# Expert layers that return half of the experts' rows by an accumulating indirect DMA into HBM instead of by one-hot products

## What is computed

```python
scores = jnp.einsum('ntd,ed->nte', x, gate_w)
probs = jax.nn.softmax(scores, axis=-1)
g, m = jax.lax.top_k(probs.transpose(0, 2, 1), k)        # each expert picks its own 128 tokens
xin = x[batch_idx, m]                                    # gather: rows of the normed x
h = jnp.einsum('nekd,edf->nekf', xin, w1)
h = jax.nn.gelu(h, approximate=False)
h = jnp.einsum('nekf,efd->nekd', h, w2)
out_tok = g[..., None] * h
out = jnp.zeros((n, t, d), dtype=x.dtype).at[batch_idx, m].add(out_tok)   # scatter: give the rows back
...
x = x + 0.5 * _L1_ffn_ref(_layernorm(x, axis=-1), ...)
```

## Time and profile before

| | us |
|---|---|
| median of 3 runs | 1667.79 (1666.23 to 1670.37) |
| the profiled execution: its own time | 1667.2 |
| its span, first to last instruction | 1665.5 |

### The profile page before, as it was taken

The page is one execution under the profiler, slowest core; times in us unless marked ns, Lnnn a source line. Parts: engine busy times, 40 slices in busy tenths (PEclk is TensorE's granted clock), DMA queues, the critical chain, the costliest instruction groups (busy, mean ns, idle before and its releaser), DMA issues. The chain is left out here.

```text
span 1665.5 us, 40705 instructions
## 1 busy us (share of the span) xinstructions
PE 1446.4 (87%) x12722; PEld 1003.0 (60%) x12722; DVE 1267.3 (76%) x3158; ACT 1160.5 (70%) x2439; POOL 778.2 (47%) x1204
## 2 busy tenths in 40 slices
PE   5999679999999999989970999999878609999998
PEld 2554334445454544435550899999745408999997
DVE  6777478888888888657848677877778586778776
ACT  5888337777777787758842778787566407887785
POOL 4687724545454444434415666554022106665540
PEclk9999759999999999989975899999989658999999
DMA  5022201111111111001012111110001101111110
GB/s 156 29 83 85 86 13 46 41 42 44 42 43 41 45 40 45 5 1 38 26 48 94 40 38 38 32 30 24 1 26 39 38 3 40 51 50 50 49 36 25
DMA packets 84640, 70.92 MB, mean 43 GB/s; under 512 B 16752, under 2 KB 78000, under 8 KB 84528
## 3 DMA queue, kind: packets, MB, share of 16 engines
q1 hardware_dynamic: 76336, 52.62, 11.3%
q0 software_dynamic: 8192, 16.79, 3.8%
HBM read 46.81 MB, written 22.54 MB: 42 GB/s over the span
## 5 line engine op out<-in xcount | busy, mean ns | idle before, releaser
L1111 DVE TENSOR_REDUCE at_negmax<-at_s_ps 128x2 f32<-128x1024 f32 (+3 forms) x384 | 389.4, 1044 | 64.7 <-PE at_s_ps L888 57.4
L1017 ACT ACTIVATE at_p<-at_x_ps 128x512 f32<-128x512 f32 x640 | 355.3, 596 | 98.9 <-PE at_x_ps L900 92.4
L1335 POOL DMA_INDIRECT e_x_in<-xn,e_row_c x256 | 259.2, 1012 | 146.0 <-issue 75.7
L1072 POOL TENSOR_SCALAR_AFFINE_SELECT at_p<-at_p 128x256 f32<-128x256 f32 (+1 forms) x448 | 191.3, 441 | 243.8 <-ACT at_p L1017 243.7
L900 PE MATMUL at_x_ps<-qr,kr 50*128 50x512 bf16 (+3 forms) x1024 | 227.4, 305 | 18.6 <-ACT at_p L1017 10.9
L1458 DVE TENSOR_TENSOR e_hid_lo<-e_hid,e_hid_hi 128x512 fp32r<-128x512 f32 x256 | 177.3, 693 | 86.8 <-ACT e_hid_hi L1422 77.2
L883 PE MATMUL at_s_ps<-kr,qr 48*128 48x512 bf16 (+3 forms) x1024 | 188.3, 312 | 18.3 <-PEq L1679 11.9
L1421 ACT ACTIVATE e_hid<-e_h_ps 128x512 f32<-128x512 f32 x256 | 154.9, 605 | 43.0 <-PE e_h_ps L1363 37.8
L916 PE MATMUL at_o_ps<-at_p,at_va 128*32 128x512 f32 (+3 forms) x2048 | 179.8, 447 | 0.0
L900 PEld LDWEIGHTS at_x_ps<-qr,kr 50*128 50x128 bf16 x1024 | 66.6, 94 | 153.6 <-ACT at_p L1017 136.8
L1363 PE MATMUL e_h_ps<-e_x_hi,w_hi 128*128 128x256 f32 x512 | 156.5, 306 | 0.0
(11 more groups left out here) (210 smaller groups left out, 3392.5 us busy)
## 6 DMA issues: line engine op xcount, KB each, us to landing
qr<-q_parts SPq DMA_DIRECT2D x128, 48.0 KB
kr<-k_parts SPq DMA_DIRECT2D x128, 48.0 KB
xres<-in_x_dram SPq DMA_DIRECT2D x8, 512.0 KB, 8.2
qr<-q_parts SPq DMA_DIRECT2D x128, 32.0 KB
xn<-m_n_xhat SPq DMA_DIRECT2D x16, 256.0 KB
e_x_in<-xn,e_row_c POOLq DMA_INDIRECT x256
xn<-sc_n_xhat SPq DMA_DIRECT2D x16, 256.0 KB
out_dram<-xres SPq DMA_DIRECT2D x16, 256.0 KB
```

Of the source, the lines that this page charges most:

```text
L1017: a.activation(p_sb[g % 2][:, i, :], x_ps[i % 2][:], ACT.Exp, scale=SCALE).then_inc(x_read, 1)
L1072: sel = gp.affine_select(out=part, in_=part, compare_op=ALU.is_ge, fill=0.0, base=0, pattern=[[0, n] for n in part.shape[1:-1]] + [[1, P]] ...
L1111: v.tensor_reduce(out, scored, AX.X, ALU.max, negate=True).then_inc(s_read, 1)
L1335: nc.gpsimd.indirect_dma_start(out=x_in[k][u][:], out_offset=None, in_=xn_dram, in_offset=bass.IndirectOffsetOnAxis(ap=row_c[k][:, u:u + 1 ...
```

## The change

In each turn the experts `k` = 0, 2, 4, 6 (`BY_DMA`) return their rows by DMA, and the experts 1, 3, 5, 7 (`BY_PE`) by one-hot products as before.

- While the tokens are chosen, SyncE writes all of `xres` to two tables in HBM, `sum_dram[0]` for the even and `sum_dram[1]` for the odd sequences (`keep_rows`: 16 DMAs of 256 KB in each expert layer).
- For an item of `BY_DMA` there is no `one_hot`, no `y_hi`, no `y_lo` and no `give_back`. VectorE writes the weighted rows as float32 to `y_row` straight from `y_ps`, and GpSimd issues two indirect DMAs with `compute_op=ALU.add` (`scatter`) that add the 128 rows of each sequence to its table. Each waits for the scatter of the same table that went before it in the turn.
- GpSimd's code is written out in full instead of looped, its gathers take the row numbers straight from `rows` (no `row_c`), and `scatter` of item q-4 stands behind the gather of item q+8 (`LAG`).
- When a turn's last scatter (`k` = 6) has landed, SyncE loads the sequence from the table back into `xres` (`reloaded`: 16 DMAs of 256 KB in each layer), and only then may VectorE add the sum of the other four experts to it. In `e2` the output's stores stand in the same queue behind it.

The core of the diff:

```diff
+BY_DMA = (0, 2, 4, 6)
+BY_PE = tuple(k for k in range(E) if k not in BY_DMA)
...
+        def keep_rows(sp):
+            for n in range(NB):
+                sp.dma_start(of_batch(n), in_chunks(n)).then_inc(sums_set, 16)
...
+                def gather(i, k):
+                    after(pool, t_full, (i - 1) * S + k + 1)
+                    for u in range(U):
+                        at = (i * U + u) * E + k
+                        nc.gpsimd.indirect_dma_start(
+                            out=x_in[k][u][:], out_offset=None, in_=xn_dram,
+                            in_offset=bass.IndirectOffsetOnAxis(ap=rows[:, at:at + 1], axis=0)).then_inc(gathered[k][u], 16)
+
+                def scatter(i, k):
+                    pool.wait_ge(yl_done, i * S + k + 1)
+                    if (i, k) == (0, BY_DMA[0]):
+                        pool.wait_ge(sums_set, NB * 16)
+                    for u in range(U):
+                        if k != BY_DMA[0]:
+
+                            pool.wait_ge(scattered[BY_DMA[BY_DMA.index(k) - 1]][u], i * 16 + 16)
+                        at = (i * U + u) * E + k
+                        nc.gpsimd.indirect_dma_start(
+                            out=sum_dram[u], out_offset=bass.IndirectOffsetOnAxis(ap=rows[:, at:at + 1], axis=0),
+                            in_=y_row[k][:, u, :], in_offset=None, compute_op=ALU.add).then_inc(scattered[k][u], 16)
+
+                LAG = 4
+                for k in range(S):
+                    gather(0, k)
+                for q in range(TU * S + LAG):
+                    if q + S < TU * S:
+                        gather(q // S + 1, q % S)
+                    if q >= LAG and (q - LAG) % S in BY_DMA:
+                        scatter((q - LAG) // S, (q - LAG) % S)
...
                 def give_back(i, k, q):
+                    if k in BY_DMA:
+                        return
                     pe.wait_ge(yl_done, q + 1)
-                    pe.wait_ge(hot_done, q + 1)
-                    if k == 0:
+                    pe.wait_ge(hot_done, i * len(BY_PE) + BY_PE.index(k) + 1)
+                    if k == BY_PE[0]:
...
                 def weigh(i, k, q):
-                    dve.wait_ge(yh_done, q + 1)
+                    if k in BY_DMA:
+                        dve.wait_ge(y_full, q + 1)
+                        dve.wait_ge(cols_done, q * 2 + 2)
+                        for u in range(U):
+
+                            after(dve, scattered[k][u], i * 16)
+                            y = v.tensor_scalar(y_row[k][:, u, :], y_ps[:, u, :], wgt_c[k % 2][:, u:u + 1], None, ALU.mult)
+                        y.then_inc(yl_done, 1)
+                        return
+                    dve.wait_ge(yh_done, i * len(BY_PE) + BY_PE.index(k) + 1)
...
                             dve.wait_ge(o_full, turn * U + u + 1)
+                            dve.wait_ge(reloaded[u], turn * 16 + 16)
                             x = xres[:, turn * U + u, :]
                             v.tensor_tensor(x, o_ps[:], x, ALU.add).then_inc(x_added, 1)
...
+                for n in range(NB):
+                    sp.wait_ge(scattered[BY_DMA[-1]][n % U], n // U * 16 + 16)
+                    sp.dma_start(in_chunks(n), of_batch(n)).then_inc(reloaded[n % U], 16)
```

More of the change, by code:

```diff
@@ L1242, in choose_tokens, with experts_layer @@
     return local, rows, weight
-def experts_layer(nc, sem, h, xres, xn_dram, probs, name, out, weights=None, next_norm=None):
+def experts_layer(nc, sem, h, xres, xn_dram, sum_dram, probs, name, out, weights=None, next_norm=None):
     U = 2
@@ L1259, in experts_layer @@
         two = lambda n, sh, d=F32R: [t(f"{n}{j}", sh, d) for j in range(2)]
-        local, rows, weight = choose_tokens(nc, lambda n, sh, d: tmp.enter_context(nc.sbuf_tensor(n, sh, d)), sem, h, probs, name, weights)
-        row_c = [t(f"row_c{k}", [K, U], U32) for k in range(S)]
+        sums_set = s("sums_set")
+        of_batch = lambda n: sum_dram[n % U][n * T:(n + 1) * T, :].rearrange("(c p) d -> p c d", p=P)
+        in_chunks = lambda n: xres[:, n, :].rearrange("p (c d) -> p c d", c=C)
+        def keep_rows(sp):
+            for n in range(NB):
+                sp.dma_start(of_batch(n), in_chunks(n)).then_inc(sums_set, 16)
+        local, rows, weight = choose_tokens(nc, lambda n, sh, d: tmp.enter_context(nc.sbuf_tensor(n, sh, d)), sem, h, probs, name,
+                                            keep_rows, weights)
         loc_c, wgt_c = two("loc_c", [K, U], F32), two("wgt_c", [K, U], F32)
@@ L1268, in experts_layer @@
         y_hi, y_lo = two("y_hi", [K, U, D]), two("y_lo", [K, U, D])
+        y_row = {k: t(f"y_row{k}", [K, U, D], F32) for k in BY_DMA}
         hot = two("hot", [K, U, T])
@@ L1324, in _ @@
             def _(pool):
[L1325 to L1337, removed]
@@ L1498, in _ @@
             def _(sp):
+                for n in range(NB):
+                    sp.wait_ge(scattered[BY_DMA[-1]][n % U], n // U * 16 + 16)
+                    sp.dma_start(in_chunks(n), of_batch(n)).then_inc(reloaded[n % U], 16)
+                    if out is not None and n % U == U - 1:
+                        for m in range(n - U + 1, n + 1):
+                            sp.wait_ge(x_added, m + 1)
+                            sp.dma_start(out[m].rearrange("(c p) d -> p c d", p=P), in_chunks(m)).then_inc(stored, 16)
                 if out is not None:
-                    with sp.Fori(0, NB) as n:
-                        sp.wait_ge(x_added, n + 1)
-                        sp.dma_start(out[n].rearrange("(c p) d -> p c d", p=P), xres[:, n, :].rearrange("p (c d) -> p c d", c=C)).then_inc(stored, 16)
                     sp.wait_ge(stored, 16 * NB)
@@ L1661, in program @@
         xn_dram = dram("xn", [NB * T, D], F32)
+        sum_dram = [dram(f"sums{u}", [NB * T, D], F32) for u in range(2)]
         xres = sb("xres", [P, NB, T], F32)
```

35 lines of the change are left out of this document (21 added, 14 removed).

## The result

| | before | after |
|---|---|---|
| median of the runs | 1667.07 us | 1706.91 us |
| lowest to highest | 1666.23 to 1670.37 | 1703.19 to 1712.06 |
| ratio, 95% interval | | 1.0239 [1.0221, 1.0257] |

The changed kernel is slower by 40 us. The forecast was 1634 us, with a range up to 1690: the time lies outside it, on the side that had 0.27.

The account below looks back on a forecast made before the run. TensorE, busy 87% of the span, was taken as the bound. Terms: -28.8 - 1.7 + 6.3 + 7.8 = -16.4 us a layer, -32.8 for both, against 1667.2: 1634 us; 8-in-10 range 1606 to 1690.

Parts of the forecast that it names:

- the scatter's issue time: GpSimd's queue: one scatter taken as 1.10 us, range 0.95 to 1.465, with 0.30 us more beside it.
- the scatter's issue is dear: Rival, GpSimd's queue at `scatter`: each 0.1 us more costs 11 us in all; gain eaten at 1.40 us; chance 0.33.
- TensorE's turn without four give-backs: TensorE's slots: 31 give-backs at 0.93 us go, 28.8 us less a layer; a turn falls from 34.6 to 30.9 us.
- The copies: Start of each expert layer: without copies of row numbers the fourth gather starts earlier, 1.7 us less a layer.
- The turn of the queue: GpSimd's queue: 16 x 1.31 + 8 x 1.40 = 32.2 us a turn, 1.3 behind TensorE; 7.8 us over turns 1 to 6.
- The first turn: VectorE's first addition waits for the reload, so TensorE's slot 15 starts late: 6.3 us, once a layer.
- Landing and reload: Behind a turn's last scatter: 3.1 us from its start to landing, then 3.0 us for SyncE's reload of 256 KB.
- SyncE's stores: Stores of `xres` into tables: about 10 us, hidden inside choosing; rival not hidden, up to 5 us a layer, chance 0.05.
- TensorE stays the bound: Rival: GpSimd's queue under 30.9 us a turn and reload in time, so both stalls go, 1606 us; chance 0.15.
- the scatter lands late: Rival, scatters waiting for the preceding expert's: waits begin over 8 us to landing; at 10 us, over 1700; chance 0.07.
- The rule weighed: GpSimd's gathers: had `e_hot` lengthened them, 3 us a layer would come back, 1628 us; the mean was kept.

Follow-up runs that it names:

- group 2: Runs side by side: changed kernel again 1711.12 us; before with loop written out 1667.9; without copies, gathers five ahead 1663.01; two experts, five ahead 1635.43.
- group 1: Runs side by side: changed kernel without reload 1710.6 us, with plain scatters 1727.21, with two experts 1680.1; kernel before without copies, loop written out 1699.6.
- group 3: Changed kernel with gathers five ahead: three experts 1695.43 us, four 1708.55, four with plain scatters 1712.67, four with 64-row adding scatters 1711.87.
- group 5: Four experts, gathers five ahead, plain 32-row scatters: 1625.91 us; kernel before without copies, 32-row gathers eight ahead: 1670.6 us.

## Why the prediction was wrong

**The step that failed is the scatter's issue time.** It was taken as 1.10 us "nearer to the mean" of a gather, with 1.465 as its upper end. It is 1.702. The prediction's own rule for it, 11 us for each 0.1 us, gives 6.0 x 11 = 66 us: 1634 + 66 = 1700, against 1706.9 measured. With the measured turn and first wait in its sum, -28.8 - 1.7 + 12.3 + 6 x (37.4 - 30.9) = 20.8 us a layer, it is 1709. And where a scatter does cost what was forecast (plain, 32 rows, 1.08 us on average), the kernel with eight of them a turn took 1626 us. The rival "the scatter's issue is dear" had the place, the point from which it decides (1.40) and even 1695 at 1.65; it had 0.33. What spoke for it, more to write for a read-and-add than for a copy, was the argument, and no row stood against it. The packets that a DMA is cut into show the size of that. The page of the changed kernel, its queue of indirect DMAs (packets, MB, share):

```profile
q0 software_dynamic: 26624, 25.19, 9.4%
```

The same with plain scatters, gathers eight ahead:

```profile
q0 software_dynamic: 12288, 25.19, 4.9%
```

The kernel before has 8192 packets for its 256 gathers, 32 each. What is left is 18432 for 128 adding scatters, 144 each, and 4096 for the plain ones, 32 each. With 64 rows an adding scatter has 80 packets and still takes 1.46 us.

Point by point:

- *TensorE's turn without four give-backs, 31 x 0.93 = 28.8 us a layer:* right. With the copies it gives 1606 us as the bound; without any scatter the kernel took 1603.5. The work was there to be saved, and was not the bound any more.
- *The copies, 1.7 us a layer:* right in size (2.9 us for both layers), in group 2. In group 1 the kernel without copies was 32 us slower than the one with them; that taking them out could cost anything was in no term.
- *The turn of the queue:* the sum was right, its input wrong: 37.4 us by the means and 37.2 measured.
- *The first turn:* VectorE waits 14.9 us and TensorE 12.3, where I had 6.3. Seven scatters at 0.60 more explain 4.2 of the difference. The rest is the queue's lateness with longer scatters beside it (up to 2.4 us), and was not taken apart.
- *Landing and reload:* right, 3.3 and 3.2 us in the piece shown for 3.1 and 3.0. The end and VectorE's `y_row` (0.342 us) were right too.
- *SyncE's stores:* hidden, as taken, though their issue takes 16.2 us in `e1` and not 10. They start at 879.4, inside choosing (200 GB/s), and `e1`'s first gather comes at 911.3 us against 912.4.
- *The rivals:* "TensorE stays the bound" needed a scatter under 0.95 us; "the scatter lands late" did not happen.
- *The rule weighed, gathers made longer by `e_hot`:* half of the `e_hot` went and nothing came back; a gather's mean rose from 1.013 to 1.037 us.

**What neither the forecast nor a rival had** is that TensorE's signals can come late beside unbroken rows of indirect DMAs, in group 1 by 13 to 15 us in each layer's first turn, in group 3 by about 7 there and more in the steady turns. The kernel without copies took 36 us more than expected with it. The changed kernel's own trace shows nothing of it: its steady turns are the queue's own sum, and in its first turns TensorE waits for the filling and then for the reload. (It has 4.4 us without TensorE between 1388 and 1423, but its `e2` issues the first gather only at 1387.3.)

**What stays open:** what sets the groups apart, and by which way TensorE's signals come late in two of them. The stopping kernel without copies and the one with full plain scatters were never run in a group without the stop, so neither the number of DMAs, nor their rows, nor how far ahead the gathers run is shown to matter. Whether the signal itself, TensorE's supply of instructions, or the records are what is late was not tested. Open too is what four experts with full plain scatters take without the stop: 1712.7 us was measured in group 3.

## What to carry to other kernels

Price an indirect DMA by its form, and where no row shows the form, let the argument on what it does move the bound: one that adds at its target took 1.7 us of GpSimd's queue against 1.0 for one that copies, whether it carried 128 rows or, nearly, 64. Moving work onto a queue pays up to the point at which the queue is level with the engine that it relieves: two experts of eight, with gathers five ahead, gave 30 us, four cost 40. When a kernel shows an effect that its edit doesn't explain, run that very kernel again beside its variants before theories are built on the difference: here two sets of variants, run apart from each other, looked like a rule of the hardware, and a stretch ahead of the first edited instruction showed that they were not. And look in the trace whether a limit ever held: five items ahead was meant as 10 gathers in a row, and it was 28.

## What the runs showed of the hardware that I had not expected

- Behind the same 12 gathers of 128 rows, 1.25 us apart, in programs that are the same up to there, TensorE's progress stopped in one group of runs (7.1 us in `e1`) and not in another. In group 1 it stood 13 to 15 us a layer beside 22 gathers in a row; beside 28 in a row (group 2) it did not.
- Eight plain scatters and 16 gathers of 128 rows a turn took 36.1 us in group 3, with releases that the trace calls "remote", where the queue's own sum is 32.5. With 32 rows in the scatters it was 32.3 us, in group 5.
- A subtraction of two SBUF tiles on VectorE took 1137 ns instead of 686 while GpSimd subtracted two SBUF tiles 8 times a turn. In 140 us VectorE's lost 30.7 us in this way, about what GpSimd's took (29.1).
- An adding scatter takes 1.63 us at the median with 128 rows and 1.46 with 64, a plain one 1.00, and 1.07 with 32. Its packets are 144 and 80 for the adding ones, 32 for the plain one of 128 rows.
